# ScalarE's second scaling for h2 stands at head 6 instead of head 4 of a batch's first head group

## The reference

```python
h = _layernorm(x) * (1 + ca) + sa
x = x + ga * attention(h)        # 16 heads, keys and values through a latent of 64, causal softmax
h = _layernorm(x) * (1 + cb) + sb    # this h is called h2 in the kernel
x = x + gb * ffn(h)              # 16 experts, each takes its 512 best tokens of all 4096, and a shared one
```

## Time and profile before

| | |
|---|---|
| median of 3 runs | 1139.32 us |
| profiled execution | 1144.72 us, span 1142.9 us |
| TensorE matmul busy | 1103.9 us, 97% |
| VectorE busy | 873.1 us, 76% |
| GpSimd busy | 675.3 us, 59% |
| ScalarE busy | 594.3 us, 52% |
| attention loop, head groups 4 to 14 | 140 to 380 us of the span |

### The profile page before, as it was taken

How to read it: one execution, slowest core, us unless ns; L and a number is a source line. 1 busy time by engine, 2 the same in 40 slices (tenths; PEclk the granted TensorE clock), 3 DMA queues, 4 the chain that set the end, 5 groups by cost and what they waited for, 6 DMA issues and landing times.

```text
span 1142.9 us, 20775 instructions
## 1 busy us (share of the span) xinstructions
PE 1103.9 (97%) x6970; PEld 836.1 (73%) x6970; DVE 873.1 (76%) x2173; ACT 594.3 (52%) x1085; POOL 675.3 (59%) x771
## 2 busy tenths in 40 slices
PE   9899999999999999999899999999999999999996
PEld 4655656656656568888878888888888888888885
DVE  5677888888887687878887788777887777887662
ACT  2357777877876663222254444544445534455441
POOL 5234586687676554443866656566565656566544
PEclk9589999999999999999999999999999999999999
DMA  6435457766867553866345554555545565445621
GB/s 203 85 80 126 112 135 179 177 146 183 188 133 172 201 179 111 271 216 172 99 147 160 136 133 123 162 135 138 140 120 157 135 156 132 118 149 135 171 56 19
DMA packets 100329, 165.37 MB, mean 145 GB/s; under 512 B 18424, under 2 KB 65016, under 8 KB 98176
## 3 DMA queue, kind: packets, MB, share of 16 engines
q1 hardware_dynamic: 83600, 137.44, 42.8%
q0 software_dynamic: 14336, 25.70, 11.8%
q10 hardware_dynamic: 2288, 0.92, 0.6%
HBM read 103.71 MB, written 34.11 MB: 121 GB/s over the span
## 4 chain that ended last, share of the span: by engine, by line
PE 62%; issue 9%; POOL 9%; DVE 8%; DMA 5%; ACT 4%; SPq 1%; ACTq 1%; POOLq 0%; DVEq 0%
PE LB L587 14%; PE MB L587 13%; PE LB L973 5%; PE MB L973 5%; PE UB L587 4%; PE LB L679 4%; PE UB L717 4%; DMA XL<-xD 2%; PE MB L974 2%; PE LB L974 2%; PE XB L587 2%; DVE junk L1382 2%; PE MB L656 2%; POOL HTl L2019 1%; POOL EO L2031 1%
## 5 line engine op out<-in xcount | busy, mean ns | idle before, releaser
L2019 POOL TENSOR_TENSOR HTl<-HF,HTh 128x512 fp32r<-128x512 f32 x156 | 217.3, 1399 | 129.5 <-ACT HTh L1132 126.4
L1382 DVE CUSTOM_DVE_ANT_0 junk<-MB,MK 128x256 bf16<-128x256 f32 (+3 forms) x512 | 220.1, 486 | 56.8 <-PE MB L656 56.0
L1900 POOL TENSOR_SCALAR_AFFINE_SELECT P<-P 128x256 f32<-128x256 f32 x256 | 99.4, 411 | 122.9 <-ACT P L1071 122.4
L2087 POOL DMA_INDIRECT out_y<-EO,IDX x64 | 100.8, 1575 | 86.1 <-DVE EO L1854 72.9
L1143 ACT ACTIVATE SIL<-LB,gbT 128x512 f32<-128x512 f32 x64 | 43.8, 684 | 185.0 <-PE LB L587 185.0
L656 PE MATMUL MB<-KS,QS 48*128 48x256 f32 (+3 forms) x512 | 130.0, 365 | 4.8 <-DVE NM L1382 2.9
L1069 ACT ACTIVATE P<-LB 128x768 f32<-128x768 f32 x128 | 103.7, 810 | 57.8 <-PE LB L679 57.8
L1132 ACT ACTIVATE HTh<-HF 128x512 fp32r<-128x512 f32 x156 | 97.7, 627 | 65.0 <-DVE HF L1737 64.9
L679 PE MATMUL LB<-QS,KS 50*128 50x256 f32 (+3 forms) x512 | 123.1, 355 | 8.6 <-ACT P L1069 5.7
L679 PEld LDWEIGHTS LB<-QS,KS 50*128 50x128 f32 x512 | 77.7, 188 | 56.1 <-issue 31.0
L1737 DVE SCALAR_TENSOR_TENSOR HF<-MB,ubT,SIL 128x512 f32<-128x512 f32 x64 | 47.7, 745 | 62.9 <-PE MB L587 28.0
(11 more groups left out here) (326 smaller groups left out, 2947.4 us busy)
## 6 DMA issues: line engine op xcount, KB each, us to landing
WR<-in_gw SPq DMA_DIRECT2D x16, 1024.0 KB, 8.0
WR<-in_uw SPq DMA_DIRECT2D x16, 1024.0 KB, 5.0
WR<-in_dw SPq DMA_DIRECT2D x16, 1024.0 KB, 5.2
QS<-ST SPq DMA_DIRECT2D x96, 128.0 KB, 3.7
KS<-ST SPq DMA_DIRECT2D x93, 128.0 KB, 4.5
hD<-h SPq DMA_DIRECT2D x8, 1024.0 KB, 7.3
XT<-hD SPq DMA_DIRECT2D x7, 1024.0 KB, 8.0
X<-in_x SPq DMA_DIRECT2D x8, 512.0 KB, 4.4
```

What stands on the lines that cost most here:

```text
L1382: m = e.tensor_tensor_reduce(junk[:, o:o + w], MB[:, o:o + w], MK[:, 512 - w:512], 1.0, -3e38, ALU.add, ALU.max, NM[:, k // 4, 4 * (k % 4) ...
L1900: m = e.affine_select(out=dd, in_=dd, compare_op=ALU.is_ge, fill=0.0, base=0, pattern=[[0, 2], [1, 128]], channel_multiplier=-1)
L2019: e.tensor_tensor(HTl[:, slot, :], hf_of(n)[:], HTh[:, slot, :].bitcast(F32), ALU.subtract).then_inc(g_ht, 1)
L2087: e.indirect_dma_start(out=out2, out_offset=bass.IndirectOffsetOnAxis(ap=IDX[x_ % 3][:, q:q + 1], axis=0), in_=EO[:, q, :], in_offset=None ...
```

## The change

The second `scale2` of a batch moves from head 4 to head 6 of the even group, on ScalarE's stream alone. `k // 6` gives 0 at k = 3 and 1 at k = 6, so that both halves are still done once.

```diff
                     if k == (2 if u == NU - 2 else 7) and old:
                         split_heads(u - 2)
-                    if k in (3, 4) and old2:
-                        scale2(b - 2, k - 3)
+                    if k in (3, 6) and old2:
+
+                        scale2(b - 2, k // 6)
                 else:
```

## The result

Over ten runs each, the changed kernel takes 1146.51 us (median) and the kernel before 1140.83; the ratio is 1.0055, with a 95% interval of 1.0037 to 1.0073, or some 6.3 us with 4.2 to 8.3. The forecast was 9.0 us slower. The time lies in the forecast's range, but 9.0 us (a ratio of 1.0079) is above the interval: so the size was too large, and the mechanism has to be checked by itself.

The account below looks back on a forecast made before the run. TensorE, hardly ever stopping, bounds the attention loop; stack stalls of 8.45 us, 0 for group 12 and 0.5 for group 14 make about 9.0 us, from 1139.3 to 1148.3 us (0.8% slower), range 1141.0 to 1154.0.

Parts of the forecast that it names:

- The wait in front of head 6: TensorE's idling before head 6, waiting for head 5's exp behind the second scaling, goes: 0.67 us a place.
- Head 7's exp late, nothing in sum: Scaling ahead of head 7's exp delays it some 0.3 us; ScalarE's side between -0.67 and +0.33 us a place, near nothing.
- Group 12: The one place with only ScalarE's side of the move, no load or stack effect: counted as 0.
- SP's shift: In groups 4, 6, 8, 10 the load of X and stack DMAs go out 4.39 us later, 5.91 in group 4.
- The stall at the stack: TensorE at head 4 of the next group, stack landing late: 1.95, 2.20, 2.12, 2.18 us from groups 4, 6, 8, 10.
- The waits at the stack: TensorE shows four waits of about 2 us for KS or QS, groups 5, 7, 9, 11; below 1 us refutes.
- Behind the stall TensorE is the late one, all others wait for its scores, and I see nothing that gives the time back.: After each late stack read, no lost time is recovered, so the four stalls count in full, 8.45 us together.
- Group 14, 0.5 us slower: No X loaded; scaling before head 7's exp makes it later, with GpSimd's normalising and ScalarE behind: 0.5 us.
- The fit for DMA times: About 2.0 us plus bytes over 436 GB/s, 2.3 us for 128 KB; would mean almost no stall; set aside against landings.
- Hidden after all: Rival, chance 0.10: stack landings become as short as the shortest, stalls 1.5 us, total 2.0 us, 1141.3 us.
- the move pays: Rival, chance 0.04: SP's shift costs nothing, 0.67 us stay won at groups 6, 8, 10, 12: -2.7, 1136.6 us.
- The load is what is waited for: Rival, chance 0.03: late X delays VectorE's statistics 0.24 us in four groups, 1.0 us together; 1140.8 us.

Follow-up runs that it names:

- experiment 5: Kernel before with the second scaling at head 5, SP's stream untouched: ratio 0.9983, 1.9 us faster than before.
- experiment 6: Kernel before with the second scaling at head 5 and SP's load of X behind D and HT, ahead of DN: ratio 0.9982, 2.1 us faster.
- experiment 1: Changed kernel with SP's load of X one head later, behind D and HT and ahead of DN: ratio 1.0014 against the kernel before.
- experiment 3: Kernel before, SP's load of X also waiting for the end of k1's copy, about 6.5 us later: ratio 1.0157, 17.9 us slower.
- experiment 8: Changed kernel with the head 6 scaling ahead of q1's copy instead of behind it: ratio 1.0023 against the kernel before, 2.6 us slower.
- experiment 4: Kernel before, SP's load of X also waiting for head 6's first exp, about 2.3 us later: ratio 1.0014, 1.6 us.
- experiment 2: Kernel before, SP's load of X also waiting for the end of q1's copy, about 4.1 us later: ratio 1.0061, 7.0 us slower.
- experiment 9: Kernel before, X in time, DN and the stack held for the next group's second-half maxima, about 3.8 us later: ratio 1.0040, 4.6 us slower.
- experiment 11: Kernel before with only the load of X late, issued behind the stack at head 7: ratio 1.0289, 32.9 us slower.
- experiment 10: Kernel before, DN and the stack held until the next group's head 2 exp, about 8.4 us later: ratio 1.0268, 30.5 us slower.

## Why the prediction was right in kind and too large

**The wait in front of head 6: right.** 0.67 us were to go. In group 8, TensorE started head 6 at 245.68 before, 2.89 us after the copy NMh of head 4, and after the change 2.14 us after it (242.62 against 240.48), 0.75 us sooner. Experiments 5 and 6 show what it is worth where nothing else happens. In experiment 5 the batches from groups 6, 8 and 10 (from one copy NMh of head 4 to the next) took 43.22, 43.25 and 43.22 us instead of 43.87, 43.86 and 43.90, 0.61 to 0.68 less each; by the medians about 2 us of the 2.7 that four places could give.

**Head 7's exp late, nothing in sum: not contradicted.** In experiment 1, ScalarE's stream is that of the change, and the kernel is 1.6 us from before, with an interval that holds 0. In the change's own trace TensorE still was 0.5 us early at head 2 of group 11 (12.48 us after NMh against 12.97), so this side gave more than the forecast's 0. Group 12, which was also counted with 0, came out faster: from its copy NMh to that of group 14 it took 40.55 us instead of 41.64. How much of that is the move is open, as the kernel before had two waits for NMl there (1.13 and 0.41 us) that the change had not.

**SP's shift: right, but for group 4.** 4.3 us instead of 4.39 in group 8. For group 4 the forecast had 5.91. There the load stood 2.11 us behind the copy NMh before (154.27 to 156.38) and 6.48 after (150.38 to 156.86), so 4.37. The forecast took the group's own timeline, in which TensorE was late because its clock was down, and I had not looked at the clock:

```profile
152.00:156.00 4.00, 3.99 (x22) 1.18 (x22) 2.38 (x11) 3.30 (x8) 2.34 (x7) 0.57 0.82 175
```

A dip stands at the same heads in the profiles of experiments 3 (0.70 between 152 and 156 us), 6 and 8 (0.57 and 0.58 between 148 and 152), and in those of the change and of experiments 1, 4 and 5 it does not. So it comes and goes between executions at this place.

**The stall at the stack: right in place, in landing and in how late the read is.** The last KS DMA took 5.3, 5.0, 5.6 and 5.6 us in groups 4, 6, 8 and 10 after the change, where the forecast had 5.0 and three times 5.6. In group 6 TensorE read the stack 20.66 us after NMh (195.26 to 215.92) and before 18.67 us (198.92 to 217.59): 1.99 us late, with 2.20 forecast. From group 8 the read came 20.92 us after NMh instead of 18.66: 2.26, with 2.12 forecast. In group 10 the pairs are 287.53 to 308.39 and 286.65 to 305.34: 2.17, with 2.18 forecast. From group 4 it is 0.92 (20.33 against 19.41), with 1.95 forecast, because of the dip.

**The waits at the stack: wrong, and by the forecast's own sign.** It had four waits of about 2 us and called itself wrong if they are below 1 us. They are 0.98, 0.99, 0.27 and 0.72. TensorE did not come to the stack early and wait, as the forecast's sum has it; other waits, which it did not have, had held it up on the way. In group 11, after the change, VectorE's statistics of the late X and behind them TensorE's wait for the maxima read:

```profile
298.69 1.41 DVE L1334 BATCH_NORM_STATS2 st<-X 128x6 f32<-128x256 f32 x4 [1.01 <-DMA X<-in_x]
...
301.18 0.44 PE L656 MATMUL MB<-KS,QS 48*128 48x384 f32 x1 [0.25 <-DVE NM L1383]
```

Counted from NMh, TensorE was 0.49 us early at head 2, 0.55 late at head 3 (16.26 against 15.71), 1.07 late when it began head 4 behind the wait for NMl (19.76 against 18.69), and 2.17 late at the stack. The stack ended last in all four places, and so it set the sum; the waits ahead of it were contained in it. That is the reason why the sum held although the waits did not. Experiments 2 and 9, in which X is nearly or wholly in time, have waits of up to 1.5 and 2.2 us for KS.

**The step that mis-sized the sum: "Behind the stall TensorE is the late one, all others wait for its scores, and I see nothing that gives the time back."** These are TensorE's heads 6 and 7 of group 11 and head 0 of group 12, first before:

```profile
310.79 0.38 PE L679 MATMUL LB<-QS,KS 50*128 50x256 f32 x1
...
313.89 0.38 PE L679 MATMUL LB<-QS,KS 50*128 50x256 f32 x1
...
316.52 0.38 PE L679 MATMUL LB<-QS,KS 50*128 50x256 f32 x1
```

and after:

```profile
313.35 0.38 PE L679 MATMUL LB<-QS,KS 50*128 50x256 f32 x1
...
316.25 0.38 PE L679 MATMUL LB<-QS,KS 50*128 50x256 f32 x1
...
319.02 0.38 PE L679 MATMUL LB<-QS,KS 50*128 50x256 f32 x1
```

The first read of the stack was 3.05 us later than before on this scale (308.39 against 305.34), head 6 is 2.56 and head 0 of group 12 2.50. So 0.55 us come back in three heads. A likely reason is ScalarE, which in the kernel before works nearly without a gap from head 2 to head 6 of the odd groups and catches up while TensorE stands. Experiment 9 gives as much back (1.59 us late at head 5 of group 11, 0.91 at head 7), but no run shows that it is ScalarE. The batch from group 10 to 12 grew by 1.51 us by the NMh copies (43.90 to 45.41) and that from group 6 to 8 by 1.36 by SP's issues of X:

```profile
201.09 0.39 SPq L334 DMA_DIRECT2D X<-in_x  x1
...
288.82 0.39 SPq L334 DMA_DIRECT2D X<-in_x  x1
```

(before, groups 6 and 10; groups 4 and 8 are in the earlier trace rows) and after:

```profile
156.86 0.39 SPq L334 DMA_DIRECT2D X<-in_x  x1
...
201.72 0.39 SPq L334 DMA_DIRECT2D X<-in_x  x1
...
294.02 0.39 SPq L334 DMA_DIRECT2D X<-in_x  x1
```

The batches are 44.71, 43.87 and 43.86 us before; after, with group 8's at 246.95, they are 44.86, 45.23 and 47.07. So the forecast's 2.2 us a batch are about 1.4 in the second and 1.5 in the fourth, with 0.2 in the first, where the kernel before had lost some time to its clock. The third, group 8 to 10, grew by 3.2 us, although TensorE's read of the stack was no later there (2.26 us) than elsewhere: 1.1 us were added between that read and head 5, which came 3.40 us late (24.82 us after NMh against 21.42). What fell there is the clock:

```profile
260.00:264.00 4.00, 2.98 (x21) 1.39 (x25) 2.18 (x9) 2.63 (x7) 1.05 (x4) 0.87 1.08 308
264.00:268.00 4.00, 4.00 (x42) 1.95 (x34) 2.23 (x10) 2.75 (x5) 2.07 (x4) 0.71 1.09 219
```

This was no term of the forecast. So 9.0 against 6.3 us is in part luck: had the third batch grown by 1.4 us like its neighbours, the loop would have lost some 4 us (an estimate from these batches), less than half of the forecast.

**What the forecast lacked ahead of the stack.** The maxima's DMA (NMl, 8 KB, ScalarE's queue) landed 6.7 us after its issue in group 9, 5.0 before, and TensorE waited 1.16 us for it. It had also been issued 0.7 us later against NMh (3.79 us behind it instead of 3.09). The busy share of the 16 DMA engines was 1.07 between 256 and 260 us, and 0.87 there before. The Trainium skill (Trainium Kernel Development and Optimization, its rules on DMA) says that queues of different engines run on the same 16 DMA engines and interleave. The longer landing fits that, but no run takes it apart from the rest: in experiments 1 and 6, with the stack in time, NMl is not waited for, and in experiment 4 it is. It cost the change little, since the wait for the stack ended behind it.

**Group 14, 0.5 us slower: wrong in sign.** From NMh of group 14's head 4 to that of group 15's head 0, the loop took 10.34 us before (372.19 to 382.53) and 9.97 after (373.49 to 383.46). I had counted what the scaling costs at head 6 and not what its leaving head 4 gives; no run takes the two apart. In experiment 1, with the same ScalarE stream, it is 9.68.

**The fit for DMA times.** The forecast set the fit of the Trainium skill (DMA: Bandwidth & Descriptors, on the two cost components) against the landings. The Trainium skill gives this fit for the path of DMAs that GpSimd issues, and KS is issued from SP, so that the landings here (3.7 us at least) neither bear it out nor refute it.

**The rivals.** "Hidden after all" and "the move pays" fell with the four waits for KS. "The load is what is waited for" is real but contained in the stall here: 3.5 us of VectorE's waits in the change. Alone, in experiment 1, it costs 1.6 us at the most likely, and in experiments 3 and 11 it is what TensorE waits for. "Hidden" was said to give no stall at a landing below 3.4 us; for group 4 the forecast's numbers would leave 0.35 us even so.

## What to carry to other kernels

Before an instruction is moved, look for who waits for its semaphore on an in-order DMA queue, and at everything written behind that wait: 1.1 us of ScalarE's work moved by two heads held 4.3 us of SP's queue, and the DMA that mattered was ten issues behind. The smallest move that frees the bottleneck was the best here (head 5 instead of head 6), since the gain is the same and lateness beyond a consumer's margin is paid. A sum can hold while the waits that it names do not: what ends last hides the waits ahead of it, so compare how late the consumer is, and not only how long it waits. And where a stall is added up from a trace, look at the granted clock in both places: a long wait can be paid a second time, 30.5 us for 22.3 us of waits in experiment 10.

## What the runs showed of the hardware

TensorE's granted clock fell to half behind the long waits of experiment 10. After one of 5.9 us it was 0.50 (1.2 GHz instead of 2.4) between 280 and 284 us, although TensorE was busy all the time. The same sixteen products of P with the values took 3.21 us there:

```profile
281.20 3.21 PE L719 MATMUL UB<-P,V 128*32 128x512 f32 x16
```

and 1.71 us in the change at 249.09. It fell behind all four stalls of experiments 10 and 11.

Behind shorter waits the length of the wait does not tell whether the clock falls. In the change, experiment 2 and experiment 9 it fell in one batch of four, each time in group 9 (0.71, 0.64 and 0.62 between 264 and 268 us). In experiment 2 that was behind a wait of 1.49 us, while one of 1.53 us in group 11 was followed by no fall. In experiment 8 it fell in group 7, behind waits of 0.57 and 0.70 us, and not in group 9, behind 1.14:

```profile
216.00:220.00 4.00, 4.00 (x26) 1.63 (x25) 2.68 (x13) 2.55 (x7) 2.41 (x4) 0.62 1.07 225
```

And in group 4 of the kernel before it fell to 0.57 where no wait of TensorE between 140 and 152 us was longer than 0.34 us. What decides stays open.
